# Grouped-query attention scores, two heads at a time on the two halves of TensorE's rows, in an iteration whose order is written anew

## The reference, cut to what matters

```python
x = _L0_xattn_ref(x, ctx_2048, w_qk, w_v, b_v, w_t, b_t)     # (32, 128, 512)
q = (x @ Wq + bq).reshape(b, l, KVH, GROUPS, HD)             # 8 x 4 heads of 16
k = ctx_2048 @ Wk + bk
scores = einsum('bkgld,bksd->bkgls', q, k) * scale + mask
out = einsum('bkgls,bksd->bkgld', softmax(scores), v)
return layernorm(out @ Wo + bo + x) * gamma + beta
```

## Time and profile before

| | |
|---|---|
| median of 3 runs | 779.62 us (779.21 to 782.26) |
| the profiled execution, its own time | 782.72 us |
| its span, first to last instruction | 780.3 us |
| granted clock of TensorE, mean | 0.98 of full speed |
| busy: PE, DVE, POOL, ACT | 92%, 78%, 75%, 59% |
| chain that ended last | PE 66%, DVE 12%, DMA 9%, issue 5% |
| moved by DMA | 101.64 MB, 130 GB/s |

### The profile page before, as it was taken

How to read it: one execution, slowest core, us unless ns; L and a number is a source line. 1 busy time by engine, 2 the same in 40 slices (tenths; PEclk the granted TensorE clock), 3 DMA queues, 4 the chain that set the end, 5 groups by cost and what they waited for, 6 DMA issues and landing times.

```text
span 780.3 us, 17141 instructions
## 1 busy us (share of the span) xinstructions
PE 716.9 (92%) x4886; PEld 579.4 (74%) x4886; DVE 608.3 (78%) x1030; ACT 463.5 (59%) x1058; POOL 582.2 (75%) x752
## 2 busy tenths in 40 slices
PE   6798979999999999999999999999999999998773
PEld 5676867888788787878778787877878787775642
DVE  5675875969789796969879696978879697885747
ACT  5655638376574937657483855747385665748161
POOL 4886488697877969787896978789697878858054
PEclk9999999999999999999999999999999999999896
DMA  8544361634527262452717254362715436251511
GB/s 321 176 123 125 92 177 55 177 99 148 138 94 191 83 179 89 152 142 89 205 68 184 88 157 129 101 191 74 200 66 171 122 116 170 81 146 61 136 37 61
DMA packets 60363, 101.64 MB, mean 130 GB/s; under 512 B 10032, under 2 KB 30128, under 8 KB 60208
## 3 DMA queue, kind: packets, MB, share of 16 engines
q1 hardware_dynamic: 59616, 101.03, 43.6%
q10 hardware_dynamic: 720, 0.27, 0.2%
HBM read 41.50 MB, written 8.39 MB: 64 GB/s over the span
## 4 chain that ended last, share of the span: by engine, by line
PE 66%; DVE 12%; DMA 9%; issue 5%; SPq 3%; POOL 2%; ACT 1%; DVEq 1%; POOLq 0%; ACTq 0%
PE banks L924 8%; PE banks L840 7%; DMA qstack<-mrep 7%; DVE maxima L1567 6%; PE banks L937 5%; PE banks L871 4%; PE banks L873 4%; PE banks L872 4%; PE banks L895 4%; PE banks L827 2%; PE banks L825 2%; PE banks L826 2%; PE banks L813 2%; SPq L403 2%; PE banks L949 2%
## 5 line engine op out<-in xcount | busy, mean ns | idle before, releaser
L1567 DVE TENSOR_REDUCE maxima<-banks 128x4 f32<-128x512 f32 x256 | 158.9, 685 | 5.9 <-PE banks L895 4.5
L1226 ACT ACTIVATE prob<-banks 128x512 f32<-128x512 f32 x256 | 135.1, 608 | 26.3 <-PE banks L924 25.0
L1592 DVE RECIPROCAL dens<-dens 128x512 f32<-128x512 f32 x30 | 100.4, 3348 | 46.6 <-DMA dens<-sides 46.6
L601 POOL TENSOR_TENSOR ta<-ta,cb_s 128x516 f32<-128x516 f32 x64 | 77.1, 1205 | 74.9 <-ACT ta L1168 74.8
L840 PEld LDWEIGHTS banks<-ta,att 128*128 128x128 f32 x1024 | 119.0, 190 | 2.7 <-POOL ta L608 0.2
L840 PE MATMUL banks<-ta,att 128*128 128x130 f32 x1024 | 119.4, 275 | 0.0
L1160 ACT ACTIVATE att<-banks,negmax 128x512 f32<-128x512 f32 x128 | 88.7, 716 | 33.7 <-DVE negmax L1517 33.6
L1210 ACT ACTIVATE qh<-banks,bq_s 128x256 fp32r<-128x256 f32 x64 | 30.7, 480 | 104.1 <-PE banks L873 104.1
L924 PE MATMUL banks<-qstack,kstack 128*128 128x512 f32 x256 | 81.4, 422 | 9.5 <-DMA qstack<-mrep 9.2
L1517 DVE TENSOR_REDUCE negmax<-banks 128x1 f32<-128x512 f32 x128 | 85.2, 685 | 3.9 <-PE banks L827 3.7
L871 PE MATMUL banks<-x2h,wq_h 128*128 128x256 f32 x256 | 74.5, 291 | 4.1 <-POOL x2l L669 4.1
(11 more groups left out here) (170 smaller groups left out, 1956.1 us busy)
## 6 DMA issues: line engine op xcount, KB each, us to landing
qstack<-qh SPq DMA_DIRECT2D x128, 128.0 KB, 2.4
xs<-in_x SPq DMA_DIRECT2D x16, 512.0 KB, 4.4
ys<-in_ctx SPq DMA_DIRECT2D x16, 512.0 KB, 3.8
et<-in_ctx_turned SPq DMA_DIRECT2D x16, 512.0 KB, 3.3
xt<-in_x_turned SPq DMA_DIRECT2D x16, 512.0 KB, 3.6
kstack<-kph SPq DMA_DIRECT2D x128, 64.0 KB, 2.0
qstack<-ql SPq DMA_DIRECT2D x64, 128.0 KB, 2.4
out_x<-late SPq DMA_DIRECT2D x32, 256.0 KB, 2.1
```

Source lines behind the costliest of these rows:

```text
L601: nc.gpsimd.tensor_tensor(part, part, cb_s[:].unsqueeze(1).broadcast_to([P, 2, CW]), ALU.add).then_inc(sem["ta_done"], 1)
L1226: nc.scalar.activation(prob[:, 2 * p + odd], banks[:, slot(plan, f"st{j}{kv}")], exp_f).then_inc(sem["prob_done"], 1)
L1567: nc.vector.tensor_reduce(maxima[:, 0, :, p, :, g].rearrange("x o j -> x j o"), banks[:, slot(plan, f"mx{g}{p}")].rearrange("x (j o s) -> ...
L1592: nc.vector.reciprocal(dens[:], dens[:]).then_inc(sem["dinv_done"], 1)
```

## The change

One matmul per head had 112 rows of which half met zeros. Now `score_pair` issues two matmuls, one on partitions 0 to 63 and one on 64 to 127, each for one head of a pair, into two banks. To bring the rows into place, the DMAs write every fourth partition (`part:P:4`): a head's 16 dimensions times three parts and the row of the maxima interleave within one half. `kstack` needs no zeros then, is filled from `kh` and `kl` directly and is half as large; `kpl` is gone, and `spread_k` keeps only `kph` for `max_scores`. The rows of the maxima move to partitions 3, 35, 67, 99. The exps are numbered n = 2p + odd, so that `values` of the even heads needs exps 0, 2, 4 and 6.

The order in the iteration is written anew on all five engines, with the table of banks.

```diff
-MROW_STEP = 8
+HALF = P // 2
+MAX_ROW, MROW_STEP = 3, 32
...
-    ("z0", 0), ("en13", 1), ("b00", 1), ("b01", 1), ("st00", 2), ("st01", 2), ("st02", 2), ("st03", 2),
-    ("st04", 2), ("k", 1), ("st05", 2), ("st06", 2), ("st07", 2), ("z1", 0), ("r0", 2), ("o00", 2), ("o01", 2),
+    ("b00", 1), ("b01", 1), ("st00", 2), ("st01", 2), ("st02", 2), ("st03", 2), ("st04", 2), ("st05", 2), ("k", 1),
+    ("st13", 2), ("st14", 2), ("st15", 2), ("st16", 2), ("st17", 2), ("v", 1), ("b10", 1), ("b11", 1), ("vt", 1),
...
-        kstack = sb("kstack", [P, 2, KV, P], F32R)
+        kstack = sb("kstack", [P, 2, KV // 2, P], F32R)
...
                     for part in (0, 2):
-                        sp.dma_start(qstack[32 * part:32 * part + 32, p].bitcast(F32),
+                        sp.dma_start(qstack[part:P:4, p].bitcast(F32),
                                      qh[32 * p:32 * p + 32].bitcast(F32)).then_inc(qstack_in[p], 16)
                 wait(sp, "ql_done", q, G - 1)
                 for p in range(KV // 2):
-                    sp.dma_start(qstack[32:64, p].bitcast(F32),
+                    sp.dma_start(qstack[1:P:4, p].bitcast(F32),
                                  ql[32 * p:32 * p + 32].bitcast(F32)).then_inc(qstack_in[p], 16)
...
-                sp.dma_start(qstack[96:P:MROW_STEP].rearrange("r p j g l -> r (p j g) l").bitcast(F32),
+                sp.dma_start(qstack[MAX_ROW:P:MROW_STEP].rearrange("r p j g l -> r (p j g) l").bitcast(F32),
...
             def stack_k(i):
-                wait(sp, "kb_done", i, 0)
-                wait(sp, "kp_done", i, 0)
+                if isinstance(i, int) and i == 0:
+                    sp.wait_ge(kstack_marked, 2)
+                wait(sp, "kl_done", i, 0)
                 wait(sp, "st_ps", i - 1, 15)
                 for p in range(KV // 2):
-                    rows, heads = slice(32 * p, 32 * p + 32), slice(2 * p, 2 * p + 2)
-                    for part, src in enumerate((kph[rows], kph[rows], kpl[rows])):
-                        sp.dma_start(kstack[32 * part:32 * part + 32, :, heads].bitcast(F32),
-                                     src.bitcast(F32)).then_inc(kstack_in, 16)
+                    rows = slice(32 * p, 32 * p + 32)
+                    for part, src in enumerate((kh[rows], kh[rows], kl[rows])):
+                        sp.dma_start(kstack[part:P:4, :, p].bitcast(F32), src.bitcast(F32)).then_inc(kstack_in, 16)
 
...
             def spread_k(i):
 
-
-                wait(pool, "kl_done", i, 0)
+                wait(pool, "kh_done", i, 0)
                 wait(pool, "mx_ps", i - 1, 15)
-                wait(pool, "st_ps", i - 1, 0)
                 shape = [P, 2, 2, P]
                 nc.gpsimd.tensor_tensor(kph[:], kh[:].bitcast(F32).unsqueeze(2).broadcast_to(shape),
                                         parity.unsqueeze(1).unsqueeze(3).broadcast_to(shape), ALU.mult
                                         ).then_inc(sem["kb_done"], 1)
-                nc.gpsimd.tensor_tensor(kpl[:], kl[:].bitcast(F32).unsqueeze(2).broadcast_to(shape),
-                                        parity.unsqueeze(1).unsqueeze(3).broadcast_to(shape), ALU.mult
-                                        ).then_inc(sem["kp_done"], 1)
 
             def add_bias(i, j, h):
...
                     split_y(i + 1, 0)
+                if s1:
+                    scale_values(i, 1)
+                if split_next:
                     split_y(i + 1, 1)
-                if s1:
-                    scale_values(i, 1)
-                    spread_k(i)
-                if s2:
-                    residual_bias(q, 0)
                 if s3:
                     scale_shift(i - 2, 0)
                 if s3 and (s1 or s2):
                     scale_shift(i - 2, 1)
                 if s2:
+                    residual_bias(q, 0)
+                    residual_bias(q, 1)
                     at_low(q, 0)
                 if s1:
                     x2_low(i, 0)
-                if s2:
-                    residual_bias(q, 1)
+                    spread_k(i)
...
-            def scores(q, plan, i, j, kv, masked):
-
-                name = f"st{j}{kv}"
-                if j == 0 and kv == 0:
+            def score_pair(q, plan, i, j, n, masked):
+
+
+                p = n // 2
+                if j == 0 and n == 0:
                     pe.wait_ge(kstack_in, (q + 1) * 16 * 3 * (KV // 2))
-                odd, p = kv // 4, kv % 4
-                if j == 0 and odd == 0:
+                    pe.wait_ge(maxrow_in, (q + 1) * 16)
+                if j == 0:
                     pe.wait_ge(qstack_in[p], (q + 1) * 16 * 3)
-                    pe.wait_ge(maxrow_in, (q + 1) * 16)
-                wait_slot(pe, plan, name, i)
-                o = banks[:, slot(plan, name)]
-                last = mm(o, kstack[:, j, 2 * p + odd], qstack[:, p, j], start=True, stop=not masked)
+                for odd in range(2):
+                    wait_slot(pe, plan, f"st{j}{n + odd}", i)
+                    rows = slice(HALF * odd, HALF * (odd + 1))
+                    last = mm(banks[:, slot(plan, f"st{j}{n + odd}")], kstack[rows, j, p], qstack[rows, p, j],
+                              start=True, stop=not masked)
+                    if not masked:
+                        last.then_inc(sem["st_ps"], 1)
                 if masked:
-                    last = mm(o, mk[:, j], ident.unsqueeze(1).broadcast_to([P, G, P]), start=False, stop=True)
-                last.then_inc(sem["st_ps"], 1)
+                    for odd in range(2):
+                        mm(banks[:, slot(plan, f"st{j}{n + odd}")], mk[:, j],
+                           ident.unsqueeze(1).broadcast_to([P, G, P]), start=False, stop=True).then_inc(sem["st_ps"], 1)
 
             def values(q, plan, i, j, odd):
 
                 name = f"o{j}{odd}"
                 if j == 0 and odd == 0:
                     wait(pe, "v2_done", q, 3)
-                wait(pe, "prob_done", q, 8 * j + 4 * odd + 3)
-                wait_slot(pe, plan, name, i, have=("prob_done", -1, 8 * j + 4 * odd + 3))
+                wait(pe, "prob_done", q, 8 * j + 6 + odd)
+                wait_slot(pe, plan, name, i, have=("prob_done", -1, 8 * j + 6 + odd))
...
                     attend(i, plan, 0, 1)
                 if s2:
-                    scores(q, plan, i, 0, 0, masked)
-                    scores(q, plan, i, 0, 1, masked)
-                    scores(q, plan, i, 0, 2, masked)
-                    scores(q, plan, i, 0, 3, masked)
-                    scores(q, plan, i, 0, 4, masked)
+                    score_pair(q, plan, i, 0, 0, masked)
+                    score_pair(q, plan, i, 0, 2, masked)
+                    score_pair(q, plan, i, 0, 4, masked)
                 if s1:
                     kv_project(i, plan, "k", 0, "k_ps")
                 if s2:
-                    scores(q, plan, i, 0, 5, masked)
-                    scores(q, plan, i, 0, 6, masked)
-                    scores(q, plan, i, 0, 7, masked)
+                    score_pair(q, plan, i, 0, 6, masked)
+                    residual_transpose(q, plan, i, 0)
                 if s0:
                     z_project(i, plan, 1)
                 if s2:
-                    residual_transpose(q, plan, i, 0)
                     values(q, plan, i, 0, 0)
                     values(q, plan, i, 0, 1)
-                    scores(q, plan, i, 1, 0, masked)
-                    scores(q, plan, i, 1, 1, masked)
-                    scores(q, plan, i, 1, 2, masked)
-                    scores(q, plan, i, 1, 3, masked)
+                    score_pair(q, plan, i, 1, 0, masked)
+                    score_pair(q, plan, i, 1, 2, masked)
+                    score_pair(q, plan, i, 1, 4, masked)
+                    score_pair(q, plan, i, 1, 6, masked)
                 if s1:
                     kv_project(i, plan, "v", 1, "v_ps")
-                if s2:
-                    scores(q, plan, i, 1, 4, masked)
-                    scores(q, plan, i, 1, 5, masked)
-                if s1:
                     attend(i, plan, 1, 0)
                     attend(i, plan, 1, 1)
-                if s2:
-                    scores(q, plan, i, 1, 6, masked)
-                    residual_transpose(q, plan, i, 1)
-                    scores(q, plan, i, 1, 7, masked)
+                    v_transpose(i, plan)
+                if s2:
                     values(q, plan, i, 1, 0)
                     values(q, plan, i, 1, 1)
-                if s1:
-                    v_transpose(i, plan)
+                    residual_transpose(q, plan, i, 1)
...
-            def exp_scores(q, plan, j, kv):
-                wait(act, "st_ps", q, 8 * j + kv)
-                odd, p = kv // 4, kv % 4
-                if p == 0:
-                    wait(act, "o_ps", q, 2 * (j - 1) + odd)
+            def exp_scores(q, plan, j, n):
+                wait(act, "st_ps", q, 8 * j + n)
+                if n < 2:
+                    wait(act, "o_ps", q, 2 * (j - 1) + n)
```

(27 more changed lines are left out.)

124 lines of the change are left out of this document (59 added, 65 removed), and 12 rows, old and new, of the table WIDE_USES.

## The result

The changed kernel takes 790.3 us (median of 4 runs, 788.62 to 791.74); the kernel before, run beside it, 780.9 (4 runs, 779.21 to 783.69). The ratio is 1.012, with an interval of 1.0075 to 1.0156: slower by 9 us, where 771.4 was forecast. The profiled execution took 788.62 us with a span of 786.8, so the traces differ by 6.5 us in span and by 5.9 in their own times, and what follows explains those 6.5.

What follows compares the result with a forecast made beforehand. PE's own work, about 44 of 45.1 us per pair, was taken as the bound. 13 intervals at 44.7 us save 5.2, the second interval 3.5, the last pair adds 0.5: -8.2 from 779.62 gives 771.4 us, range 756 to 786.

Steps and rivals of the forecast that it cites:

- Start of the pair to m: From the pair's first work to max_spread (m): 24.04 us, 23.8 with DVE ahead, 24.3 with the seam; m just in time.
- m to the scores: From max_spread to the first score: maxima's DMA lands in 2.4 us, scores start at 4.35, PE waits 0.4 us.
- Rival 4: Maxima's DMA stays at 3.7 us, so ys ahead was not the cause; 791 us, chance 0.08.
- k's bank: Bank of k, released by DVE's second layer0_out step: ready at 5.3 against PE's 5.2, a 0.1 us wait.
- Scores to `v`: From the first score to v: ACT's exps, normalise, sums and residual set the pace; v starts 12.9 us after m.
- `v` to the next pair: v, attend, values, v_transpose and residual transposes on PE: 7.45 us, ending 20.4 after m against 21.94 before.
- Scores in pairs: Two 64-row matmuls cost 0.27 us per pair of heads, eight 2.2; PE loses 1.8 us of work per pair of batches.
- inside what I count: Score matmuls: the array's drain at a change of tiling mode is already held in the 0.27 us per pair.
- Seam: POOL's steps before q_project at the next pair's start: within 0.5 us either side, counted as 0.25 us.
- the tail: Last pair: values wait for three more exps per batch and sums come one exp later, +0.5 us.
- Rival 3: POOL's at_high chain 1 us later than placed delays q_project and m in every pair; 784.5 us, chance 0.13.
- Second interval: The interval at 106.19, which lost 3.30 us to the maxima's DMA behind ys, gets 3.5 us back.

Runs made afterwards that it cites:

- ys_early: Kernel before, with the next pair's ys load issued ahead of the copies into qstack; ratio 0.998.
- order_only: Changed kernel in its new order, with the old full-height scores, zeroed copies kph and kpl, and old rows of the maxima; ratio 1.013 to the kernel before.
- rows4: pool_seam with the four rows of the maxima on partitions 51, 59, 67 and 75; ratio 0.992 to the kernel before.
- full_pool: rows4_pool's order of work with order_only's full-height scores, kph and kpl, and old rows of the maxima; ratio 1.010 to the kernel before.
- rows4_pool: rows4 with POOL's second gamma and beta product moved behind the residual's bias and at_low; ratio 0.994 to the kernel before.
- pool_seam: Changed kernel with two POOL steps, the second residual_bias and spread_k, moved behind x2_low(q,1); ratio 1.001 to the kernel before.
- one_group: Kernel before with the four rows of the maxima on neighbouring partitions 96 to 99; ratio 1.040.
- same_half: pool_seam with both matmuls of a pair on the same partitions 0 to 63; ratio 1.032 to the kernel before.

## Why the prediction was wrong, step by step

- *Start of the pair to m.* 24.3 forecast, 24.39 measured (447.02 to 471.41). `mrep` was to end at t = 1.7, it ended at 1.74, and m waits for nothing: right.
- *m to the scores.* The step that failed in every pair: "the nearest row without such a load is `qstack<-qh`, 2.4 us". The landing was 3.37 us, the scores began at 5.14, not 4.35. Half of it was right (`ys` ahead did cost time: at least 0.57 us by ys_early, 3.76 against 2.61 in order_only, where more was moved), but that row was another form, on many partitions, and the change also moved the four rows to places that fill more slowly: +0.76 against order_only, of which rows4 gave 0.52 back by their places alone. Rival 4 had the symptom, a long landing, and the wrong cause. This step was the first of several: with it mended in rows4, two terms stood in the way that the walk had at 0.1 us or not at all. k's bank waits for DVE's `ta` (0.1 forecast, 0.39 to 0.64 there), and DVE's product and a POOL step hold each other up; in after the product ends at m + 20.2 whenever it starts. No run reached 44.7 in its median period; the best has 44.83.
- *Scores to `v`.* `v` at 12.9, measured 13.38. ACT's chain was as walked (first exp to exp 7), and took up 0.3 of the 0.8. From the scores to the next pair 16.05 forecast, 15.90 measured.
- *`v` to the next pair.* 7.45 forecast, 7.66 measured, 0.08 of it the first matmul of `v` behind the pairs (0.19 from 439.36 to the next start, for 0.12).
- *Scores in pairs.* 0.27 a pair of heads was right inside a block (0.23), and the ends of a block were not in it. The last pair takes 0.41 to 0.43 us to the next matmul, some 0.1 more goes by ahead of the first and 0.06 to 0.08 behind; in the block of eight another 0.3 is lost to ACT's sum. Three blocks cost 0.94 + 0.42 + 1.53 = 2.9 us from their first start, where eight times 0.27 is 2.2, and the three ways in and out come on top. Against full height six scores in a block save some 0.4 us, eight save 0.4, and a single pair costs 0.1 more than its two scores did. Where the prediction sets 0.27 beside the earlier trace rows as what the trace shows, it is its own estimate. Taking the named waits out of the interval, PE's work went from 44.0 to 43.85 us; order_only's is 44.35 and full_pool's 44.0 against rows4_pool's 43.3. So the pairs saved some 0.5 to 0.7 us, where 1.8 was written, and the new order gave 0.35 back. (This remainder is rough: it is 43.5 in rows4's long iterations and 43.05 in its short ones, with the same matmuls.) The Trainium skill's drain (TensorEngine Tiling (Array Packing), Key Properties) was dismissed as "inside what I count"; the trace agrees with the page in that each change of form costs time that 0.27 a pair doesn't hold, some 0.3 us for the way in and out together.
- *Seam.* In the steady iteration within 0.2 us (pool_seam gained 0.18), as said. In the tail, +0.5 forecast and +5.0 measured, the same two POOL steps cost 3.4 (47.55 to 44.19 us without them), part of it as low clock. Rival 3 named the mechanism and looked for it in the wrong stretch, where PE has other matmuls to do; in the last full interval there are none.
- *Second interval.* 3.5 us back forecast, 2.64 came.

In sum: 8.0 us for eleven periods that are 0.73 too long, 0.7 for the two others, 4.5 for the tail, 0.9 for the second interval and 0.75 for the start come within 0.2 us of the 14.7 between -8.2 and +6.5.

Not shown: why a change of form costs what it does, whether the hold-up of DVE and POOL costs the total anything, why rows4 (2.85 us) lands 0.24 later than order_only with as many ports, and why the clock falls in some of the like iterations of one_group and same_half and not in others.

## What to carry to other kernels

A DMA into a few partitions is priced by where they lie: when a layout moves such rows, look at their landing again, also where the bytes are the same. Give the last iterations their own walk, since a step that hides behind other matmuls in the steady state is bare there and the low clock adds to it. Change the form of the array in large blocks: six or eight matmuls in half height gained, a lone pair and single ones between other work lost. And look at the starts of the single matmuls before a mean is called their price: here the mean of 0.38 us was 0.23 and the ends of the block.

## What was not expected of the hardware

- The same 64 KB to four partitions took 2.61 to 5.32 us by place and by the load ahead.
- DVE's product of two SBUF operands (0.69 us) took 1.77 when a POOL step had begun 0.06 us before it, and POOL's 1.28 us step took 1.76 when DVE had begun 0.08 before. A tenth of a microsecond decided over 0.95 us of an iteration. In after it ended at the same time after m as in pool_seam and in long iterations of rows4 (m + 20.2 to 20.3), whenever it started.
- Two matmuls on different halves of the rows start within 0.04 us of each other, and such pairs follow each other every 0.23 us, like single full-height ones.
- The clock fell to half behind 1.8 to 2.1 us of idle time in six of one_group's eleven intervals, and behind 1.2 to 1.7 in six of same_half's; the same 1.2 to 1.6 us in after never did it in the steady part. The length of one idle stretch did not decide.
